# First part of a later piece copied by ScalarE, and its residual taken two ring events later

## What is computed

```python
latent = x @ Wc_down                                   # 4096 x 128
q = (latent @ Wq_up).reshape(Bsz, Tlen, N_HEAD, HEAD_DIM)
kv = latent @ Wkv_up
k, v = (kv[..., :HEAD_DIM], kv[..., HEAD_DIM:])
att = jnp.einsum('bthd,bsd->bhts', q, k) * scale
att = jnp.where(causal[None, None], att, -jnp.inf)
att = jax.nn.softmax(att, axis=-1)
y = jnp.einsum('bhts,bsd->bthd', att, v).reshape(Bsz, Tlen, C)
return y @ Wc_proj
```

## Time and profile before

| | |
|---|---|
| median of 3 runs | 1002.3 us (1002.26 to 1006.01) |
| profiled execution | 1003.18 us, its span 1001.3 us |
| TensorE matmul, busy share of the span | 87% |
| VectorE | 70% |
| ScalarE | 53% |
| GpSimd | 30% |

### The profile page before, as it was taken

One profiled execution on the slowest core, in us unless ns is written; L12 is line 12 of the kernel. 1 busy time (PEld: TensorE's weight loads), 2 busy tenths in 40 slices (PEclk: granted clock), 3 DMA queues, 4 the chain that ended last, 5 costly groups with the idle time before them and its releaser, 6 DMA issues. The chain is left out here.

```text
span 1001.3 us, 20703 instructions
## 1 busy us (share of the span) xinstructions
PE 869.1 (87%) x5630; PEld 522.3 (52%) x5631; DVE 700.3 (70%) x2447; ACT 535.6 (53%) x909; POOL 301.6 (30%) x565
## 2 busy tenths in 40 slices
PE   5768999999999999999999658851999999999994
PEld 3322333333333333333333147741999999999993
DVE  6457788888888888888886137856466666666652
ACT  3502566666666665666666513311566565656561
POOL 1201223333233322333323223313134344343311
PEclk9955999999999999999999977955899999999998
DMA  9330011111111111211000156742011001001000
GB/s 337 115 103 11 9 52 51 48 45 37 53 58 48 48 33 46 67 44 51 24 25 18 38 200 215 223 132 74 15 31 34 31 31 34 26 33 32 17 16 7
DMA packets 54739, 62.88 MB, mean 63 GB/s; under 512 B 12526, under 2 KB 45958, under 8 KB 54544
## 3 DMA queue, kind: packets, MB, share of 16 engines
q1 hardware_dynamic: 50928, 53.67, 16.1%
q0 software_dynamic: 3744, 8.40, 2.6%
HBM read 35.86 MB, written 9.55 MB: 45 GB/s over the span
## 5 line engine op out<-in xcount | busy, mean ns | idle before, releaser
L595 ACT ACTIVATE PR<-ST 128x1024 f32<-128x1024 f32 (+1 forms) x256 | 239.4, 969 | 144.0 <-PE ST L517 144.0
L648 DVE CUSTOM_DVE_ANT_0 junk<-ring,causal 128x384 bf16<-128x384 f32 (+3 forms) x512 | 222.2, 486 | 43.6 <-PE ring L486 38.1
L486 PE MATMUL ring<-K,Q 96*128 96x512 bf16 (+3 forms) x768 | 206.1, 343 | 35.1 <-DVE R L620 10.7
L651 DVE TENSOR_REDUCE MP<-ring 128x1 f32<-128x512 f32 x256 | 164.0, 681 | 36.4 <-PE ring L486 36.2
L517 PE MATMUL ST<-Q,K 99*128 99x512 bf16 (+3 forms) x768 | 181.1, 332 | 8.7 <-DMA Q<-MT 6.9
L762 POOL TENSOR_SCALAR_AFFINE_SELECT PR<-PR 128x512 f32<-128x512 f32 x96 | 61.2, 637 | 300.1 <-ACT PR L595 295.5
L1439 PE MATMUL hp<-XNT,WS 128*128 128x128 f32 x1248 | 148.5, 278 | 2.4 <-DVE XNT L1511 2.4
L1439 PEld LDWEIGHTS hp<-XNT,WS 128*128 128x128 f32 x1248 | 148.0, 195 | 4.9 <-DVE XNT L1511 3.0
L486 PEld LDWEIGHTS ring<-K,Q 96*128 96x128 bf16 x768 | 70.6, 99 | 138.3 <-DVE MP L651 37.5
L1447 PE MATMUL yp<-W2s,HT 128*128 x624 | 141.2, 379 | 0.7 <-DVE z L1523 0.7
L517 PEld LDWEIGHTS ST<-Q,K 99*128 99x128 bf16 x768 | 59.5, 98 | 138.2 <-issue 46.9
(11 more groups left out here) (173 smaller groups left out, 901.2 us busy)
## 6 DMA issues: line engine op xcount, KB each, us to landing
Q<-T SPq DMA_DIRECT2D x192, 64.0 KB, 2.6
W1s<-in_L_ffn_W_dram SPq DMA_DIRECT2D x8, 1024.0 KB, 12.1
W2s<-in_L_ffn_W_dram SPq DMA_DIRECT2D x8, 1024.0 KB, 7.3
Y<-in_L_attn_x_dram SPq DMA_DIRECT2D x8, 512.0 KB, 6.8
Y<-W1s SPq DMA_DIRECT2D x32, 128.0 KB
XQ<-in_L_attn_x_dram SPq DMA_DIRECT2D x8, 512.0 KB, 3.6
x_rows<-XQ SPq DMA_DIRECT2D x8, 512.0 KB, 7.4
W1s<-den_rows SPq DMA_DIRECT2D x15, 256.0 KB
```

Of the source, the lines that this page charges most:

```text
L486: last = pe.matmul(bank[:, at:at + w], Q[0:NR, g, i // BW, h, i % BW * P:(i % BW + 1) * P], K[b % 2][0:NR, k * NQ:k * NQ + w], start=True, ...
L595: act.activation(PR[t % RB][:, heads[0]:heads[-1] + 1, off:NQ], unit_of(ST[(NU * n + u) % 2], s), ACT.Exp, scale=SCALE).then_inc(exp_done, 1)
L648: op = dve.tensor_tensor_reduce(junk[:, done % 2, at:at + w], src, causal[:, NQ - w:NQ], 1.0, LOWEST, ALU.add, ALU.max, dst)
L651: op = dve.tensor_reduce(dst, src, AX, ALU.max)
```

## The change

ScalarE, not VectorE, now rounds the product of a later batch's piece to part 1. The copy stands in ScalarE's queue right behind the exponential of the first unit of the piece's step. VectorE's own copy is gone, and its subtraction comes behind event k + 2, where it came behind event k + 1. The bank counts follow.

```diff
@@ -138,8 +138,8 @@
 for event in range(len(EVENTS)):
     if EVENTS[event][0] != "piece":
         DONE.append(event)
-    if event and EVENTS[event - 1][0] == "piece":
-        DONE.append(event - 1)
+    if event > 1 and EVENTS[event - 2][0] == "piece":
+        DONE.append(event - 2)
 DONE_AT = [DONE.index(event) + 1 for event in range(len(EVENTS))]
@@ -565,6 +565,12 @@
+            def first_part(b, name):
+                k = EVENTS.index(("piece", b, name))
+                act.wait_ge(ring_ready, k + 1)
+                parts_sent(act, b, name)
+                act.activation(parts(name)[0], ring[k % RING][0:rows_of(name), :], ACT.Copy).then_inc(part1, 1)
+
@@ -594,6 +600,9 @@
                         act.activation(PR[t % RB][:, heads[0]:heads[-1] + 1, off:NQ], unit_of(ST[(NU * n + u) % 2], s),
                                        ACT.Exp, scale=SCALE).then_inc(exp_done, 1)
+                        for name in PIECES:
+                            if (g, s) == PIECES[name] and u == UNIT_AT[s] and b < B - 1:
+                                first_part(b + 1, name)
@@ -607,10 +616,6 @@
-            def piece(k, b, name):
-                parts_sent(dve, b, name)
-                dve.tensor_copy(parts(name)[0], ring[k % RING][0:rows_of(name), :]).then_inc(part1, 1)
-
@@ -673,10 +678,8 @@
                     elif kind == "values":
                         values(k, a)
-                    else:
-                        piece(k, a, b)
-                    if k and EVENTS[k - 1][0] == "piece":
-                        residual(k - 1)
+                    if k > 1 and EVENTS[k - 2][0] == "piece":
+                        residual(k - 2)
```

## The result

The changed kernel takes 1008.9 us (median of 7 runs, 1008.1 to 1010.3) against 1002.3 us before. The ratio is 1.0056, with a 95% interval of 1.0041 to 1.0071: slower, by 4 to 7 us. A second set of runs gave 1008.5 us and 1.0045 (1.0027 to 1.0063). Whether it is more than 0.5% slower is open. Forecast was 0.46% slower than the kernel before; the two ratios say 0.56% and 0.45%.

A forecast was written before the change was run, and what follows sets the result against it. TensorE in its order was taken as the bound, with stops where the ring is not free. Later subtractions of 2.72 + 1.16 + 0.71 = +4.6 us on the 1002.3 us median gave 1006.9 us, range 1004 to 1009.5.

The forecast's parts named there:

- The place and the mechanism: Around each piece: VectorE's subtraction ends later, delaying TensorE's event k + 3 and all behind it; 0.20 us at `q00`, batch 2.
- The size at a piece: At each piece, the subtraction comes later: +0.20 us at 14 of 18 places, +0.36 us at `k1`.
- the handover of 0.03 us: Between TensorE ending an event's matmuls and VectorE starting on it: 0.03 us added.
- no slack: At `q00` of batch 2, TensorE's event k + 3: a subtraction 0.20 us later makes it 0.20 us later.
- `q00` of batch 1: Piece where the granted clock is at half: subtraction starts at 95.55 instead of 94.84, +0.71 us.
- One sign: TensorE's matmul waits for the subtraction were to rise from 10.7 us by 4 to 5 us.
- a step of the granted clock behind attention: Behind attention the clock falls and rises again; its rise against the experts' later start can move the end a us or two.
- the forecast's 4.6: Sum of the later subtractions over all three batches: 2.72 + 1.16 + 0.71 = +4.6 us.
- VectorE as the bound: Rival on VectorE's queue: the casts' 10.8 us come off, 991.5 us, or about 997 if half does; chance 0.05.
- Nothing moves: Rival: TensorE's slack or a wait further on swallows the later subtraction; 1002 to 1004 us, chance 0.12.
- ScalarE's late copy: Rival: copy starts late or holds the next exponential, up to 0.57 us each; 1017 us at worst, chance 0.15.

The follow-up runs named there:

- late-only: Kernel before, VectorE still casting part 1 but subtracting two events behind the piece: 1024.6 us, ratio 1.0211; repeated, 1022.5 us, 1.0193.
- copy-only: Changed kernel, ScalarE still copying part 1, but VectorE subtracting one event behind the piece as before: 999.8 us, ratio 0.9962 against the kernel before.

## Why the prediction was right, and where it was short

**The place and the mechanism** were right. The subtraction ends later although VectorE does less, TensorE's event k + 3 moves with it, and VectorE idles 0.48 us behind it. The two halves alone have opposite signs: copying on ScalarE gains 0.38%, subtracting an event later costs about 1% at full clock; in the change they don't cancel. At full clock subtracting later costs a query group 1.16 us and the whole change costs it 0.46, so taking the cast away gives back 0.70 for two pieces: 0.35 us of the cast's 0.60, because event k + 1 isn't there yet.

**The size at a piece** was a little short. Of the sum's terms, the handover of 0.03 us is the one mis-sized. Behind the piece's own matmuls, event k + 1 starts on TensorE at 223.38 and ends, by its row, at 223.76; VectorE takes it at 223.85, 0.09 us later; at `k1` the same step is 0.10 us (262.46 to 262.56). That makes the subtraction at `q00` 0.26 us later in place of 0.20. Event k + 3 is only 0.22 us later, because the prediction's "no slack" was not quite so: where TensorE waits for a subtraction, event k + 3 starts 0.06 us behind its end (233.59 and 233.65 in the earlier trace rows, 225.73 and 225.79 now), and at `q00` before it was 0.10, so 0.04 us was slack. The groups grew by 0.46, 0.62 and 0.47 us where the prediction had 0.40, 0.56 and 0.40: 0.03 us more a piece, 0.5 us over all 18. For `q00` of batch 1 it had 0.71 us; in the second profile of the change the subtraction starts at 96.67 and k + 2's matmuls end at 95.94, 0.73 us apart, where before both fell at 94.84.

One sign was missed: TensorE's matmul waits for the subtraction were to rise by 4 to 5 us and rose by 3.3. The prediction let all 18 pieces count there, but only 10 places stop the matmuls: `q01`, `k1` and `q11` of each batch, 3 x (0.23 + 0.39 + 0.23), and `q00` of batch 1, 0.74 us (0.74 to 1.48).

**What was missing** is half clock inside the loop. The prediction looked for a step of the granted clock behind attention alone. In the first profile of the change two stretches behind longer stops cost about 2.6 us, in the second there are none. In that second one the groups from the first to the last begin 472.5 us apart (79.82 to 552.34), before 467.4 (78.72 to 546.09): 5.1 us, 0.5 above the forecast's 4.6. The groups from 1 to 15, at full clock in both, give 4.1 us of it (forecast 3.7); the rest is group 0, in which the clock also rises from half. This is the cost of the change without the stretches. It lies inside both measured intervals (4.1 to 7.1 us and 2.7 to 6.3 us), so the medians do not show that half clock adds to the change's time; for the late-only kernel that was shown. Nor do the 2 us between 1006.9 and 1008.9 need it. Part of them is the base: the forecast stands on 1002.3 us, and the kernel before, run beside the later kernels, had medians of 1003.9 to 1004.3. Medians are a coarse measure here. From group 15's beginning to the end of the span the two late-only profiles, of equal programs, take 454.6 and 449.7 us, while undisturbed groups repeat to 0.01 us.

**The rivals.** VectorE as the bound is refuted by copy-only: 18 operations less on VectorE with the subtraction left in its place, and 0.38% (3.8 us) gained, not 10.8 us. "Nothing moves" is refuted by the groups. ScalarE's late copy is refuted by leaving it out and by doubling it. The Trainium skill (Perfetto Trace Analysis, Optimizing Tensor Performance, Matmuls) asks for banks that rotate so that evacuation overlaps matmuls. The 0.48 us that VectorE idles behind each subtraction is the overlap given up, and the trace agrees with the direction; the net cost of a piece was less, 0.23 us for a query piece and 0.39 us for `k1`, as the cast's time paid for part.

**A version that beats both**: keep the copy on ScalarE and leave the subtraction one event behind the piece (e1_copy_only), 999.8 us, 0.24 to 0.51% faster than before.

## What to carry to other kernels

When an operation is taken off an engine, ask what that engine finds next: work removed where the next input is not yet made becomes waiting, not time. In a ring of three banks, freeing a bank two events late empties the ring, and the producer's next event then starts in lockstep with the release; count the order of release before the number of operations. A stop on TensorE can cost more than its length, since the matmuls behind it may run at half clock; a few matmuls that nobody reads can be worth their time there, as they were in the late-only kernel (10 us) and were not shown to be in the change itself.

## Unexpected about the hardware

- Stops of 1.4 us on TensorE in a loop that is otherwise dense were sometimes followed by half clock for the next microseconds (2 of 9 in one profile of the change and in that of the doubled copy, none in the other profile of the change and in that without the copy). Stops of 1.6 to 2.0 us were in 7 of 9 cases in each of the two profiles of late-only, and stops of 0.80 us in copy-only and of 1.0 to 1.17 us in the kernel before never in their profiles. With four more matmuls in the stop none was seen. The two stretches of the change cost 1.06 and about 1.5 us, by the groups they fell in.
- VectorE took a 512-column bf16 event 0.09 us behind the end of its row when it came right behind the f32 matmuls of a piece, and 0.04 us behind it at event k + 3 (226.22, the matmul's row from 225.79 for 0.39 us). The ends of TensorE's rows are modelled, so this need not be a difference of the true ends.
